# The seventh stage of an eight-stage transformer kernel: output product per group of four heads, queries in halves, stacks of 128 rows loaded a step or more earlier

## What is computed

```python
qp = q @ Wq.T
kv = latent_kv @ Wkv_expand.T
k, v = jnp.split(kv, 2, axis=-1)            # 16 heads of 32 features
scores = jnp.einsum('bhqd,bhkd->bhqk', qh, kh) * inv_sqrt_d
scores = jnp.where(causal, scores, jnp.finfo(scores.dtype).min)
attn = jax.nn.softmax(scores, axis=-1)
out = jnp.einsum('bhqk,bhkd->bhqd', attn, vh)
return out @ Wout.T                         # x = x + tanh(g_xattn[3]) * this
```

## Time and profile before

| | |
|---|---|
| median of 3 runs | 4096.8 us (4094.54 to 4097.43) |
| the profiled execution's own time | 4098.23 us |
| its span in the trace | 4096.5 us |
| TensorE busy | 2674.5 us, 65% |
| VectorE busy | 2534.1 us, 62% |
| ScalarE busy | 1655.7 us, 40% |
| GpSimd busy | 619.0 us, 15% |
| mean granted clock of TensorE | 0.799 of full |

### The profile page before, as it was taken

One profiled execution on the slowest core, in us unless ns is written; L12 is line 12 of the kernel. 1 busy time (PEld: TensorE's weight loads), 2 busy tenths in 40 slices (PEclk: granted clock), 3 DMA queues, 4 the chain that ended last, 5 costly groups with the idle time before them and its releaser, 6 DMA issues.

```text
span 4096.5 us, 42393 instructions
## 1 busy us (share of the span) xinstructions
PE 2674.5 (65%) x12196; PEld 2077.1 (51%) x12196; DVE 2534.1 (62%) x4354; ACT 1655.7 (40%) x3214; POOL 619.0 (15%) x2159
## 2 busy tenths in 40 slices
PE   3330604234140466998989989653898847999999
PEld 2220503223030455665656656542777745888887
DVE  5679697887979632565655656554665553444443
ACT  1108173553759202443434434212555522333332
POOL 0006152332516100000000000001222221000000
PEclk7565756666575775998989989756999978999999
DMA  3000000000000026111111101002222214222332
GB/s 139 2 16 0 0 0 0 0 0 0 0 12 0 16 89 235 50 55 48 67 52 50 69 33 67 17 0 64 57 53 50 54 40 150 97 96 96 103 111 75
DMA packets 68555, 211.29 MB, mean 52 GB/s; under 512 B 12572, under 2 KB 13852, under 8 KB 61284
## 3 DMA queue, kind: packets, MB, share of 16 engines
q1 hardware_dynamic: 65892, 201.56, 14.6%
q0 software_dynamic: 2560, 8.42, 0.5%
HBM read 162.72 MB, written 22.05 MB: 45 GB/s over the span
## 4 chain that ended last, share of the span: by engine, by line
issue 29%; PE 29%; DVE 7%; ACT 3%; SPq 2%; DMA 1%; POOL 1%; POOLq 0%; ACTq 0%; DVEq 0%; PEldq 0%
PE ps L87 9%; PE ps L89 8%; PE ps L88 8%; SPq L468 2%; DVE c_junks L1039 2%; ACT c_junks L166 1%; DVE g_pT_lo L1308 1%; PE ps L1627 1%; ACT g_p L768 1%; PE ps L1647 1%; DMA g_q<-g_q_lo 1%; PE ps L1773 1%; PE ps L1785 0%; PE ps L1574 0%; POOL h_sorted L569 0%
## 5 line engine op out<-in xcount | busy, mean ns | idle before, releaser
L166 ACT ACTIVATE b_junk_high<-b_z,b_tk 128x2048 bf16<-128x2048 f32 x208 | 414.7, 1994 | 212.1 <-POOLq L172 151.8
L158 DVE TENSOR_SCALAR_CACHE_REDUCE b_junk_low<-b_z,b_tk 128x2048 bf16<-128x2048 f32 x208 | 471.8, 2341 | 1.7 <-POOLq L175 1.7
L1526 PE MATMUL ps<-ident,b_z 128*128 128x128 f32 x256 | 42.5, 337 | 560.5 <-DVEq L946 533.4
L1526 PEld LDWEIGHTS ps<-ident,b_z 128*128 128x128 f32 x256 | 39.6, 180 | 564.3 <-DVEq L946 535.2
L669 ACT ACTIVATE e_p<-ps,e_st 128x512 f32<-128x512 f32 x256 | 175.9, 687 | 253.2 <-DVE e_st L1087 253.2
L130 POOL TENSOR_TENSOR ln_rstd<-ln_var,minus_half 128x4 f32<-128x4 f32 x24 | 24.7, 1029 | 1547.9 <-DVE ln_var L115 1524.3
L1103 DVE TENSOR_TENSOR e_pT_lo<-ps,e_pT_hi 128x512 fp32r<-128x512 f32 x256 | 175.4, 686 | 132.3 <-ACT e_pT_hi L679 132.3
L1087 DVE TENSOR_REDUCE e_st<-ps 128x1 f32<-128x512 f32 x256 | 175.8, 687 | 113.1 <-PE ps L89 105.7
L136 PE MATMUL ps<-ident,xn 128*128 128x128 f32 x320 | 72.8, 422 | 244.0 <-DVE xn L118 244.0
L136 PEld LDWEIGHTS ps<-ident,xn 128*128 128x128 f32 x320 | 65.5, 227 | 252.9 <-DVE xn L118 252.9
L143 ACT ACTIVATE xT_hi<-ps 128x512 fp32r<-128x512 f32 x80 | 47.8, 597 | 352.9 <-PE ps L136 352.6
(11 more groups left out here) (456 smaller groups left out, 8378.3 us busy)
## 6 DMA issues: line engine op xcount, KB each, us to landing
h_w<-in_l_blob SPq DMA_DIRECT2D x80, 512.0 KB, 3.6
e_g<-e_g_kept SPq DMA_DIRECT2D x32, 1024.0 KB, 4.8
e_qkw<-e_qkw_kept SPq DMA_DIRECT2D x32, 640.0 KB, 5.6
h_w<-in_l_blob SPq DMA_DIRECT2D x80, 256.0 KB, 2.6
e_g_kept<-e_g SPq DMA_DIRECT2D x8, 1024.0 KB, 5.9
g_k<-g_k_hi SPq DMA_DIRECT2D x128, 64.0 KB, 2.0
g_q<-g_q_hi SPq DMA_DIRECT2D x128, 64.0 KB, 2.0
e_blob<-in_l_heads SPq DMA_DIRECT2D x4, 1728.0 KB, 9.2
```

The lines of the kernel that those rows point to most:

```text
L158: dve.tensor_scalar(junk[j], data[:, j, :], cand[:, j:j + 1], 0.0, ALU.is_ge, ALU.add, accum_out=cnt[:, j:j + 1])\
L166: act.activation(junk[j], data[:, j, :], ACT.Sign, bias=cand[:, j:j + 1], accum_out=cnt[:, j:j + 1])\
```

## The change

- `y` is made per group and per tile: three matmuls of one group into bank 7, added to X at once. The loop has one such unit in slot two of every step (of the group before), 64 units of 3 matmuls in place of 16 of 12. `g_oT` keeps two groups in place of four.
- `q` is computed in two halves of 256 tokens, in slot one of the third and the fourth step, and for the group after the next; `k` moves to slot one of the second step. `v` stays in the first step. Four `y` of the last group remain after the last head.
- Ahead of the loop now stand k and q of groups 0 and 1; the scores of head 0 wait for all of these.
- `t` of the next batch move to slot two of steps 7 and 8, and both slots of step 9.
- The stacks have 128 rows; GpSimd fills the upper 32 with zeros once. TensorE's wait for the zeros moves to just ahead of the first scores.

```diff
-        g_q3, g_k3 = m("g_q3", [G_TERMS, 2, 4, S], F32R), m("g_k3", [G_TERMS, 2, 4, S], F32R)
+        g_q3, g_k3 = m("g_q3", [P, 2, 4, S], F32R), m("g_k3", [P, 2, 4, S], F32R)
...
-        g_oT_hi, g_oT_lo = m("g_oT_hi", [P, C, S], F32R), m("g_oT_lo", [P, C, S], F32R)
+        g_oT_hi, g_oT_lo = m("g_oT_hi", [P, 2, S], F32R), m("g_oT_lo", [P, 2, S], F32R)
...
-                    if kind in "qk":
-                        g = i * C + m_
+                    if kind == "k" or (kind == "q" and m_ == 1):
...
-                for v in g_vs:
-                    pool.memset(v.bitcast(F32), 0.0).then_inc(sem("zeros"), 1)
+                for v in (*g_vs, *(x[G_TERMS:P, :, :, :].rearrange("p u h s -> p (u h s)") for x in (g_q3, g_k3))):
+                    k(pool.memset(v.bitcast(F32), 0.0))
+                pool.sem_inc(sem("zeros"), 4)
...
-                        if i or m_:
-                            act.wait_ge(sem("g_q3"), G_STACKED * (i * C + m_))
-                        act.activation(g_q_hi[:, :], ps[:, bank, :], ACT.Copy, scale=G_SCALE).then_inc(sem("g_unit_hi"), 1)
+                        if g and not m_:
+                            act.wait_ge(sem("g_q3"), G_STACKED * g)
+                        act.activation(g_q_hi[:, G_HALF[m_]], ps[:, bank, 0:S // 2], ACT.Copy, scale=G_SCALE).then_inc(sem("g_unit_hi"), 1)
...
                     if kind == "y":
-                        n = i * TB + m_
+                        n = g // C * TB + m_
+                        if g % C:
+                            dve.wait_ge(sem("g_unit"), G_INDEX["y", g - 1, m_] + 1)
                         dve.wait_ge(sem("g_unit_ps"), u + 1)
                         dve.scalar_tensor_tensor(X[:, n, :], ps[:, bank, :], tg[:, 3:4], X[:, n, :], ALU.mult, ALU.add).then_inc(sem("g_unit"), 1)
...
                     if kind == "q":
                         pe.wait_ge(sem("g_unit"), G_INDEX["t", i, TB - 1] + 1)
                         for c in range(C):
-                            t = mm3(pe, ps[:, bank, :], g_wq_hi[:, c, q], g_wq_lo[:, c, q], xT_hi[:, c, :], xT_lo[:, c, :], c == 0, c == C - 1)
+                            t = mm3(pe, ps[:, bank, 0:S // 2], g_wq_hi[:, c, w], g_wq_lo[:, c, w], xT_hi[:, c, G_HALF[m_]], xT_lo[:, c, G_HALF[m_]],
+                                    c == 0, c == C - 1)
...
                     if kind == "y":
-                        pe.wait_ge(sem("head_out"), G_HEADS_BEFORE + C * (i + 1))
-                        for c in range(C):
-                            t = mm3(pe, ps[:, bank, :], g_oT_hi[:, c, q], g_oT_lo[:, c, q], g_wo_hi[:, c, :], g_wo_lo[:, c, :], c == 0, c == C - 1)
+                        q = slice(m_ * P, (m_ + 1) * P)
+                        pe.wait_ge(sem("head_out"), G_HEADS_BEFORE + g + 1)
+                        t = mm3(pe, ps[:, bank, :], g_oT_hi[:, g % 2, q], g_oT_lo[:, g % 2, q], g_wo_hi[:, g % C, :], g_wo_lo[:, g % C, :], True, True)
...
-    units = [("k", 0, 0), ("k", 0, 1)] + [("t", 0, m) for m in range(TB)] + [("q", 0, 0)]
+    units = [("k", 0, 0)] + [("t", 0, j) for j in range(TB)] + [("q", 0, 0), ("q", 0, 1), ("k", 1, 0), ("q", 1, 0), ("q", 1, 1)]
     first, slots = len(units), []
+    turned = {7: ((), (0,)), 8: ((), (1,)), 9: ((2,), (3,))}
     for n in range(G_HEADS):
-        i, step = divmod(n, G_BATCH)
-        one, two = [], []
-        if step % 4 == 0:
-            one.append(("v", i, step // 4))
-            if n + 4 < G_HEADS:
-                two.append(("q", (n + 4) // G_BATCH, (step // 4 + 1) % C))
-        if step % 4 == 3 and n + 5 < G_HEADS:
-            one.append(("k", (n + 5) // G_BATCH, (step // 4 + 2) % C))
-        if i and 1 <= step < TB:
-            if step == 1:
-                one.append(("y", i - 1, 0))
-            two.append(("y", i - 1, step))
-        if i + 1 < B and 9 <= step < 12:
-            if step == 10:
-                one.append(("t", i + 1, 1))
-            two.append(("t", i + 1, (0, 2, 3)[step - 9]))
+        (i, step), g = divmod(n, G_BATCH), n // 4
+        one = [(("v", g, 0), ("k", g + 2, 0), ("q", g + 2, 0), ("q", g + 2, 1))[n % 4]]
+        if n % 4 and g + 2 >= G_HEADS // 4:
+            one = []
+        two = [("y", g - 1, n % 4)] if g else []
+        if i + 1 < B and step in turned:
+            for units_, rows in zip((one, two), turned[step]):
+                units_ += [("t", i + 1, j) for j in rows]
...
-    units += [("y", B - 1, j) for j in range(TB)]
+    units += [("y", G_HEADS // 4 - 1, j) for j in range(TB)]
```

More of the change, by code:

```diff
@@ L454, in _ @@
                     g_ctx_load(i)
-                for u, (kind, i, m_, bank) in enumerate(G_UNITS):
-                    if u == G_INDEX["q", 0, C - 1]:
+                for u, (kind, g, m_, bank) in enumerate(G_UNITS):
+                    if u == G_INDEX["q", C - 1, 1]:
                         g_ctx_load(B - 1)
-                    if kind in "qk":
-                        g = i * C + m_
+                    if kind == "k" or (kind == "q" and m_ == 1):
                         src, dst = {"q": ((g_q_hi, g_q_hi, g_q_lo), g_q3), "k": ((g_k_hi, g_k_lo, g_k_hi), g_k3)}[kind]
@@ L745, in g_unit_scalar @@
                 def g_unit_scalar(u):
-                    kind, i, m_, bank = G_UNITS[u]
+                    kind, g, m_, bank = G_UNITS[u]
                     if kind == "y":
@@ L771, in _ @@
                 g_ctx_scalar(0)
-                act.wait_ge(sem("zeros"), 3)
+                act.wait_ge(sem("zeros"), 5)
                 for u in range(G_FIRST):
@@ L790, in _ @@
                     if n % 4 == 3:
-                        act.wait_ge(sem("head_ps"), G_HEADS_BEFORE + n // 4 + 1)
-                        act.activation(g_oT_hi[:, n // 4 % C, :], ps[:, 6, :], ACT.Copy).then_inc(sem("g_oT_hi"), 1)
+                        g = n // 4
+                        act.wait_ge(sem("head_ps"), G_HEADS_BEFORE + g + 1)
+                        if g >= 2:
+                            act.wait_ge(sem("g_unit_ps"), G_INDEX["y", g - 2, TB - 1] + 1)
+                        act.activation(g_oT_hi[:, g % 2, :], ps[:, 6, :], ACT.Copy).then_inc(sem("g_oT_hi"), 1)
                 end_stage(act, 6)
@@ L1256, in g_unit_vector @@
                     if kind == "q":
-                        dve.scalar_tensor_tensor(g_q_lo[:, :], ps[:, bank, :], G_SCALE, g_q_hi[:, :].bitcast(F32),
+                        dve.scalar_tensor_tensor(g_q_lo[:, G_HALF[m_]], ps[:, bank, 0:S // 2], G_SCALE, g_q_hi[:, G_HALF[m_]].bitcast(F32),
                                                  ALU.mult, ALU.subtract).then_inc(sem("g_unit"), 1)
@@ L1327, in _ @@
                         dve.wait_ge(sem("g_oT_hi"), n // 4 + 1)
[L1328 removed]
+                        dve.tensor_tensor(g_oT_lo[:, n // 4 % 2, :], ps[:, 6, :], g_oT_hi[:, n // 4 % 2, :].bitcast(F32), ALU.subtract)\
                             .then_inc(sem("head_out"), 1)
@@ L1734, in _ @@
                 pe.wait_ge(sem("weights"), READY["g"])
-                pe.wait_ge(sem("zeros"), 3)
                 def g_unit_tensor(u):
-                    kind, i, m_, bank = G_UNITS[u]
-                    q = slice(m_ * P, (m_ + 1) * P)
+                    kind, g, m_, bank = G_UNITS[u]
+                    i, w = g // C, slice(g % C * P, (g % C + 1) * P)
                     if u in G_UNIT_AFTER:
@@ L1742, in g_unit_tensor @@
                     if kind == "t":
-                        pe.wait_ge(sem("ln_xn"), TB * ln_turn("g", i) + m_ + 1)
+                        pe.wait_ge(sem("ln_xn"), TB * ln_turn("g", g) + m_ + 1)
                         for c in range(C):
@@ L1790, in g_values_tensor @@
                     if hh == 0:
-                        pe.wait_ge(sem("g_unit"), G_INDEX["v", i, g] + 1)
+                        pe.wait_ge(sem("g_unit"), G_INDEX["v", n // 4, 0] + 1)
                         pe.wait_ge(sem("head_out"), G_HEADS_BEFORE + n // 4)
@@ L1804, in _ @@
                 pe.wait_ge(sem("g_unit"), G_FIRST)
+                pe.wait_ge(sem("zeros"), 5)
                 g_scores_tensor(0)
@@ L1893 @@
 G_TERMS, G_STACKED = 3 * G_HD, 3 * 4 * 16
+G_HALF = (slice(0, S // 2), slice(S // 2, S))
 G_HEADS_BEFORE = B * E_HEADS
```

12 lines of the change are left out of this document (6 added, 6 removed).

## The result

The changed kernel takes 4029.05 us, the median of 4 runs (4027.05 to 4030.76). The kernel before, run beside it, takes 4095.67 us (4 runs, 4089.34 to 4097.43). The ratio is 0.9838, with an interval of 0.9826 to 0.9851, so the change makes the program 1.6% faster. The forecast was 4041 us in a range of 4018 to 4070.

A forecast was written before the change was run, and what follows sets the result against it. TensorE was taken to set the stage's pace, losing 60 us standing and more to a granted clock of 0.92. Terms summed to -55.7 us from 4098.2, giving 4042.5, stated as 4041 us for the runs' median, range 4018 to 4070.

The forecast's parts named there:

- stacks earlier: In the loop, query stacks made earlier land in time, so all 34.7 us of TensorE's DMA waits go.
- value part: TensorE's waits for the value product's low part: 15 at 0.31 us, 4.7 in place of 13.0, -8.3 us.
- key part: Key unit followed by a unit of the same bank: 0.54 us a pair, 13 times instead of 6, +3.8 us.
- turned tiles: Tiles behind output products or the key in steps 7 to 9 add waits: 21.0 less 3.3 us, +17.7 us.
- update of X, halves, rows: 48 more updates fit VectorE's gap, query halves keep the same columns, 128 rows uncover no weight loads: nothing each.
- end: 36 output matmuls leave the end of the stage and fill TensorE's waits in the last three steps, about -2 us.
- the start: Ahead of the loop, group 1's key behind the turned tiles brings the first scores earlier, about -9 us.
- clock: TensorE's half-clock cost in the stage, 36.5 us, falls to 3.1 plus 10.2: -23.2 us; bounds 0 or 12 stretches.
- the stacks arrive in time: Loop's query stacks: 7 us to spare forecast; the rival of late stacks, 4095 us or so, had chance 0.03.
- VectorE did not become the bound: Rival: VectorE's extra work overflows its gap, 6.4 to 6.6 us a step, +18 us, 4059 us; chance 0.09.
- Bank 7 did not block every step: Rival: X's update holds bank 7 against the next step's unit, 1.6 us x 60 = 96, 4137 us; chance 0.04.
- The rows of a stack: 128 rows in the scores' stacks: forecast 0; rival, equal rows uncover weight loads, 21 us, 4020 us, chance 0.08.

The follow-up runs named there:

- e2: The kernel before with only the query unit made earlier, for the group after the next, and turned tiles moved to steps 7 to 9; 4048.64 us, ratio 0.9881.
- e1: The changed kernel with the stacks back at 96 rows and without the zero fills; 4036.55 us, ratio 0.9848.
- e3: The kernel before with only the order ahead of the loop changed: group 1's key unit after the turned tiles and group 0's query; 4088.83 us, ratio 0.9981.
- e4: The changed kernel with the output product back to 12 matmuls per tile and batch, in steps 1 to 3; 4023.04 us, ratio 0.9821.
- e7: The changed kernel with both reorderings, those of e5 and e6, together; 4025.48 us, ratio 0.9836 to before not claimed: measured 0.9828.
- e5: The changed kernel with X's update put between the third and fourth row maximum where a turned tile stands behind it; 4027.11 us, ratio 0.9837.
- e6: The changed kernel with the key's high and low parts taken by ScalarE and VectorE ahead of the third turned part; 4026.73 us, ratio 0.9836.
- e8: e4 with one output unit a step in steps 0 to 3, one tile a step in 7 to 10, halves awaiting their own tiles; 4012.79 us, ratio 0.9790.
- e9: e8 with half of the first query stack's twelve DMAs issued by ScalarE's queue; 4012.60 us, ratio 0.9794.
- e10: The changed kernel, output product still per group, with e7's reorderings, one tile a step and halves awaiting their own tiles; 4017.51 us, ratio 0.9809.

## Why the prediction came out as it did

Where each term came out. The waits are those of TensorE in the loop; the clock is counted from 2845.0 in the kernel before, as in the prediction, and from 2830.0 in the kernel after, both some 1.9 us behind the first scores:

| step of the prediction | forecast, us | measured, us |
|---|---|---|
| stacks earlier | -34.7 | -34.7 |
| value part | -8.3 | -6.7 (13.0 to 6.3) |
| key part | +3.8 | +2.4 (3.1 to 5.5) |
| turned tiles | +17.7 | +14.2 (3.3 to 17.5) |
| update of X, halves, rows | 0 | 0 |
| end | -2 | -2.3 |
| the start | -9 | -10.8 |
| clock | -23.2 | -29.4 (36.5 to 7.1) |
| sum | -55.7 | -67.3 |
| not placed | | +2.3 |
| ahead of the stage and behind it | 0 | -6.2 |
| own time | -55.7 | -71.2 |

The row ahead of the stage and behind it is chance, and it flatters the pair of profiled executions. In the medians the change takes off 66.6 us, where I had forecast 55.8.

**Right.** The main mechanism held: the stacks arrive in time and no DMA is waited for in the loop. e2 shows that this part, with the tiles moved for it, is worth 47.8 us of the stage, 27.6 in waits and 19.3 in clock. VectorE did not become the bound, with 0.49 us of its gap left in the rows of a step with `v`. Bank 7 did not block every step. The rows of a stack and the fills cost and bring nothing (e1). Halves cost nothing: a 256-column matmul follows the next at 0.12 us. This is read from the pace and was not tried alone. The end gave 2.3 us, as the two waits for the turned weights' low part at the end of the stage (2.3 us before) no longer occur.

**Mis-sized: the clock, by 6.2 us.** The step that failed took six of twelve new waits to a cold stretch of 1.7 us. One in twelve did: the eighth of the nine waits for X's update is followed by the half clock (TensorE in order of time in the kernel after).

```profile
3114.96 0.66 PE L1749 MATMUL ps<-ident,xn 128*128 128x128 f32 x4 [1.28 <-DVE X_rows L1254]
3115.37 0.64 PE L87 MATMUL ps<-g_pT_hi,g_v_hi 128*128 128x512 f32 x1
3115.81 0.63 PE L88 MATMUL ps<-g_pT_lo,g_v_hi 128*128 128x512 f32 x1
3116.24 0.63 PE L89 MATMUL ps<-g_pT_hi,g_v_lo 128*128 128x512 f32 x1
```

512 columns follow each other at 0.43 us, the pace of the 1.2 GHz level. Behind the like wait of 1.29 us at 2885.64 the granted clock stays at 1.00 (half-microsecond windows of the same kernel, one behind each of the two waits):

```profile
3115.50:3116.00 0.50, 0.50 (x4) 0.41 (x3) 0.00 (x0) 0.35 (x1) 0.00 (x0) 0.53 0.00 0
...
2886.50:2887.00 0.50, 0.50 (x4) 0.41 (x3) 0.03 (x1) 0.43 (x1) 0.00 (x0) 1.00 0.40 98
```

So the length of a wait alone doesn't decide. Nor is it chance alone: in both repeats of this kernel it is the same eighth wait again. My price of four in nine came from the kernel before, and it doesn't carry over to another order of work. That so few came is luck as far as the forecast goes: e1, whose rows have the same pace, has four such stretches. The start went the other way: its cold stretch is 5.35 us, from 2830.0 to 2842.5, and not 3.1.

**Mis-sized: the turned tiles, by 3.5 us.** All twelve waits came at their places. Those behind `k` are 1.6 us each (1.7 forecast), `y` behind a tile waits 0.37 (0.5), and those behind X's update are 1.28 to 1.30 rather than 1.6, in step 7 as in steps 8 and 9. Counted from the end of the low part ahead of it, `y` ends at 1.02 us and not 0.85, and the tile starts at 2.30 us and not 2.45. In part that is only how the trace counts: the last matmul of `y` is modelled to end 0.16 us after the pace of the next one would begin, and VectorE's records overlap by some 0.08 us each.

**Mis-sized: key and value part.** For the key part I counted 13 pairs and had three of them among the turned tiles as well; ten pairs at 0.55 are 5.5 us. For the value part the first wait is 1.4 us, the last 0.7, and the other thirteen are 0.32, as I had priced them.

**Mis-sized: the start, by 1.8 us.** The first scores came 21.2 us after the stage's first matmul. The query stack's first DMA goes out 10.95 us after that matmul (2817.90) where it went out at 23.0 (2834.06), so it is 12.05 us earlier and not the 10 that I took. The two halves of group 1 cost 1.2 us against my 1.4, which is luck, for by my own price of a half they are 2.8 us of TensorE, and they cost it at another place. TensorE was through them at 2820.0 and stood 8.22 us. But the high part of group 1's first half waits on ScalarE until group 0's stack has landed, and the first scores wait for all units. ScalarE and VectorE in order of time in the kernel after:

```profile
2826.97 0.66 ACT L756 ACTIVATE g_q_hi<-ps 128x256 fp32r<-128x256 f32 x2 [6.99 <-DMA g_q<-g_q_lo]
...
2827.38 0.75 DVE L1262 SCALAR_TENSOR_TENSOR g_q_lo<-ps,g_q_hi 128x256 fp32r<-128x256 f32 x2 [6.68 <-ACT g_q_hi L756]
```

VectorE ends at 2828.13, and the first scores start at 2828.19. The view names a key stack's DMA for that wait; by these rows it is the low parts that end it. e3, which has no queries of group 1 ahead of the loop, has its first scores 1.2 us earlier, at 20.0 us.

**What I gave the wrong credit.** The prediction has no term in which the spread of `y` loses as such, and two in which it gains (shorter waits for the value part, the end). e4 puts it right: the output product per group costs the stage 9.7 us, since 64 updates pass through bank 7 in place of 16 and nine tiles queue behind them. The forecast held all of these waits, in the +17.7, but booked them to the tiles' place and not to the unit ahead of them. What shortens the value part's waits is for the most part not `y` either. TensorE in order of time at the same place, the values of a group's first head, in e2_early_only:

```profile
2952.89 0.50 PE L87 MATMUL ps<-g_pT_hi,g_v_hi 128*128 128x512 f32 x1 [1.65 <-DVE g_v_lo L1263]
```

and in e4_y_by_batch:

```profile
2936.28 0.50 PE L87 MATMUL ps<-g_pT_hi,g_v_hi 128*128 128x512 f32 x1 [0.60 <-DVE g_v_lo L1264]
```

No `y` stands in the step before either. In e2 that step holds `k`, 0.7 us of TensorE's work, and in e4 a query half, 1.4 us; the wait is 1.05 us shorter. Where the step before has a `y` as well the wait is 0.31 us in e2 (at 2987.04), 0.32 in e4 (2971.47) and 0.32 in the changed kernel. By this the prediction's rule, that the wait shrinks with the length of the step before, stands. Most of the shortening comes with the query half and the last 0.3 us with `y`: e4's waits for the value's low part are 8.8 us in 15 (7.8 and 1.0 in two rows of its view), against 6.3. e2 and e4 differ in the halves and in `k`'s place together, so the share of each is argued and was not tried alone.

**What stays open.** Stretches of half clock in the loop are frequent in before, e2 and e3, and there are one to four of them in after and its repeats, e1 and e7; e4, e5, e6, e8, e9 and e10 have none, with waits of up to 1.6 us among theirs (three of that length in e5). No run tells what makes one such wait cost 1.7 us and the next nothing. 2.3 us of the stage's account are not placed. A matmul behind a wait is followed after 0.34 us and not 0.23, which no row of waits counts, and there are more short waits than before; that is argued and not tried.

## What to carry to other kernels

A transfer that is waited for costs twice when TensorE's clock falls behind the wait: here the stacks' 34.7 us of waiting carried 26.6 us of half clock with them, and making one unit a few steps earlier (with the turned tiles moved for it) brought back 47.8 us of the 61.3, without the rest of the change; most of the difference went to longer waits for the value part and the half clock behind them. Count what passes through a shared bank: a unit split in four shares its columns, but brings four evictions and four places where the next unit must wait, so one long unit a step and only one does better than many short ones. Undo each part of a change that worked; here the part in its name was a loss of 10 us, and the kernel without it, with one unit of the bank a step, takes 4012.8 us for 4032.1. It also spreads the tiles and lets each half wait for its own two, which the kernel with `y` per group tried as well (4017.5 us).

## What the runs showed of the hardware

- Waits of 1.2 to 1.7 us are followed by half clock in some cases and not in others of the same length: four of nine in the value part before (1.2 us), six of eight in e2 (1.65 us), one of the twelve waits of turned tiles after, none in six of the experiments. Most such stretches cost 1.5 to 1.7 us; one each in e1, e2 and e7 cost 2.9 to 3.1.
- 96 and 128 rows of weights have the same pace, 0.32 us from score to mask. The 0.32 us at which 64 rows follow 128 in the fifth stage says nothing of rows: the next matmul there, 64 rows behind 64, comes 0.34 us later (TensorE in order of time in the kernel before, shown below). The Trainium skill (TensorE: Matmul & The Clock Gate, Part 2, Step-by-step) says that the row count doesn't matter for a weight load. The runs agree for 96 and 128 rows, and no row here speaks against it.

```profile
2481.36 0.39 PE L88 MATMUL ps<-e_qk_lo,e_qk_hi 64*128 64x512 f32 x1
```

- A queue needs 0.63 us to issue a DMA of 64 KB between two places of SBUF, with 2.0 us from issue to landing. A second queue took 3.7 us off a stack of twelve.
- The work ahead of the stage, the same in all kernels here, took between 2804 and 2812 us from one execution to the next. A gain of less than that must be read inside the stage.
